# Attention and feed-forward in one program per engine: feed-forward tiles of 128 times of one batch, and their first steps placed in the last attention cycles

## What is computed

```python
x = _layernorm(x + attention(x))        # 16 heads, latent 32, rope, causal softmax over 512 times
x = _layernorm(x + fp4_ffn(x))          # h = silu(q(x) @ q(w_gate).T) * (q(x) @ q(w_up).T);  q(h) @ q(w_down).T, width 704
x = _layernorm(x + recurrence(x))       # tanh state over the 512 times, in order
x = _layernorm(x + channel_mix(x))      # x, and x one time earlier
```

## Time and profile before

| | us |
|---|---|
| median of 3 runs (lowest, highest) | 2320.34 (2317.63, 2322.99) |
| the profiled execution's own time | 2320.48 |
| its span | 2318.7 |
| PE, DVE, ACT, POOL busy in the span | 2209.4, 1706.9, 1060.6, 1187.8 |
| mean granted TensorE clock | 0.979 |

### The profile page before, as it was taken

The page is one execution under the profiler, slowest core; times in us unless marked ns, Lnnn a source line. Parts: engine busy times, 40 slices in busy tenths (PEclk is TensorE's granted clock), DMA queues, the critical chain, the costliest instruction groups (busy, mean ns, idle before and its releaser), DMA issues. The chain is left out here.

```text
span 2318.7 us, 90879 instructions
## 1 busy us (share of the span) xinstructions
PE 2209.4 (95%) x36556; PEld 1542.3 (67%) x36556; DVE 1706.9 (74%) x4854; ACT 1060.6 (46%) x2707; POOL 1187.8 (51%) x1674
## 2 busy tenths in 40 slices
PE   6999999999999999959999999997999999997997
PEld 3556665556655555536777777776888888885775
DVE  3788888888887777749999999982555555454997
ACT  2656565655666665532222222231444444442444
POOL 3555555655555555525666666662444444441333
PEclk8999999999999999989999999997999999998999
DMA  2211111111111111120100000100101011011232
GB/s 92 91 56 64 57 65 65 65 63 58 57 64 65 65 61 60 52 69 22 33 32 32 32 32 32 34 20 29 32 32 36 32 34 33 32 32 46 84 95 77
DMA packets 101627, 117.73 MB, mean 51 GB/s; under 512 B 10672, under 2 KB 80080, under 8 KB 101456
## 3 DMA queue, kind: packets, MB, share of 16 engines
q1 hardware_dynamic: 101456, 115.44, 15.1%
HBM read 48.29 MB, written 33.55 MB: 35 GB/s over the span
## 5 line engine op out<-in xcount | busy, mean ns | idle before, releaser
L1474 ACT ACTIVATE r_state<-ps_state 128x64 f32<-128x64 f32 x1024 | 228.6, 223 | 295.8 <-PE ps_state L1573 290.7
L1570 PE MATMUL ps_state<-r_state,later_pairs_a 64*64 64x32 f32 x8192 | 334.4, 219 | 19.4 <-ACT r_state L1474 12.5
L1570 PEld LDWEIGHTS ps_state<-r_state,later_pairs_a 64*64 64x64 f32 x8192 | 295.2, 135 | 79.2 <-issue 60.7
L1573 PE MATMUL ps_state<-r_state,later_pairs_a 64*64 64x32 f32 x8192 | 334.6, 220 | 2.8 <-issue 2.8
L423 DVE CUSTOM_DVE_ANT_0 ps_near<-ps_near,mask 128x512 f32<-128x512 f32 (+1 forms) x512 | 270.5, 589 | 89.5 <-PE ps_near L519 89.3
L295 POOL TENSOR_SCALAR_AFFINE_SELECT probsT<-probsT 128x512 f32<-128x512 f32 x256 | 159.8, 636 | 271.2 <-ACT probsT L406 168.0
L1573 PEld LDWEIGHTS ps_state<-r_state,later_pairs_a 64*64 64x64 f32 x8192 | 288.8, 135 | 3.1 <-issue 3.1
L423 DVE CUSTOM_DVE_ANT_0 ps_far<-ps_far,mask 128x384 f32<-128x384 f32 (+1 forms) x512 | 198.3, 457 | 32.7 <-PE ps_far L519 31.7
L1158 POOL TENSOR_TENSOR f_fp<-f_rounded,f_scale 128x960 f32<-128x960 f32 (+2 forms) x67 | 117.3, 1750 | 166.2 <-DVE f_rounded L1248 166.2
L527 PE MATMUL ps_far<-Q,K 32*128 32x256 f32 (+2 forms) x1536 | 180.9, 415 | 1.2 <-ACT probsT L403 0.5
L1181 ACT ACTIVATE f_silu<-ps_gate 128x704 f32<-128x704 f32 x64 | 48.5, 758 | 288.5 <-PE ps_gate L1273 288.5
(11 more groups left out here) (213 smaller groups left out, 5401.1 us busy)
## 6 DMA issues: line engine op xcount, KB each, us to landing
q_swap<-q_sin SPq DMA_DIRECT2D x128, 128.0 KB, 2.1
k_swap<-k_sin SPq DMA_DIRECT2D x128, 128.0 KB, 2.1
xT<-in_xT_dram SPq DMA_DIRECT2D x16, 512.0 KB, 3.6
xtok<-in_x_dram SPq DMA_DIRECT2D x16, 512.0 KB, 3.8
x_rows<-x SPq DMA_DIRECT2D x16, 512.0 KB, 2.9
f_x<-x_rows SPq DMA_DIRECT2D x64, 128.0 KB, 2.0
x_rows<-f_x SPq DMA_DIRECT2D x64, 128.0 KB, 1.7
r_x<-x_rows SPq DMA_DIRECT2D x64, 128.0 KB, 2.1
```

Of the source, the lines that this page charges most:

```text
L1474: nc.scalar.activation(state[:, j % 2, banks, :, t, 0, :], sums[:, j % 2, banks, :, now], ACT.Tanh).then_inc(state_ready[t], 1)
L1570: nc.tensor.matmul(sums[half(v), j % 2, stays, c, now], A[half(v), 3 * q, c, :], last[half(v), stays, c, :], start=False, stop=True, skip_ ...
L1573: out = nc.tensor.matmul(sums[half(1 - v), j % 2, changes, c, now], A[half(v), 3 * q + 1 + was, c, :], last[half(v), changes, c, :], start ...
```

## The change

What it does:

1. One block for both layers. Each of the two functions now returns its five programs; `Steps` holds the place that an engine has reached in the feed-forward steps, and `feed.to(n)` writes out the steps up to n-1 where it is called inside the attention program. The barrier between the two layers, and SP's wait for all x1 stores ahead of it, are gone. x1 is read under the attention's own semaphore `x1_stored`.
2. A tile is now 128 times of one batch: tile n is times 128(n//16) to 128(n//16)+127 of batch n%16. So the first 16 tiles need one finished batch each, and tiles 0 to 7 can be loaded long before the attention ends. The rows of a tile in x1 and x2 now lie 16 KB apart (before: 1 KB, one after another); the 128 pieces of a load or store are 1 KB each in both.
3. The first feed-forward steps go to these places:
   - SP: steps -4 to 3 (8 loads of x) in cycle 62; later loads wait for z and for `x1_stored`.
   - DVE: steps -4 to -1 in cycle 63 behind y; step 0 at the end of cycle 64, step 1 of cycle 65, step 2 of cycle 67 (behind the second half of z), then the statistics of batch 15, then step 3 and on.
   - POOL: steps -4 and -3 ahead of the first mask of cycle 63, -2 and -1 behind it; steps 0 to 2 at the end of cycle 65, and behind them the norm of batch 15.
   - ACT: step -1 (copy of xT) ahead of the far Exps of cycle 63, step 0 behind them; steps 1 and 2 at the end of cycle 65, and behind them x1 of batch 15; step 3 behind that.
   - PE: step -1 (turn of x) ahead of the far scores of cycle 63; step 0 in cycle 64 ahead of the last PV, after the Exps of far[0] and far[1] (its up product waits for all Exps); step 1 in cycle 65 ahead of the output projections; step 2 in cycle 67 after all of z.
4. PSUM: `ps_hT` takes the place of near[0] and near[1], `ps_down` near[2], `ps_xT` near[3], `ps_gate` far[0] and far[1], `ps_up` far[2] and far[3]. The last half projection goes to near[2] instead of near[1], and no longer waits for the first half of z.
5. The tensors of the attention are laid out in another order, so that those of the feed-forward layer lie on ones no longer in use. SP's feed-forward steps are written out instead of looped. The weights of the later layers are loaded in step 12 instead of step 0.

The diff without what is only indented anew (the order of the SBUF tensors, which carries nothing of the text below, is left out too):

```diff
+class Steps:
+    def __init__(self, engine, step, tiles, unroll, lead, lag):
+        self.engine, self.step, self.tiles, self.unroll = engine, step, tiles, unroll
+        self.at, self.end = -lead, tiles + lag
+    def to(self, end):
+        unroll = self.unroll
+        while self.at < end:
+            if self.at == unroll and end >= self.tiles - unroll > unroll:
+                with self.engine.Fori(1, self.tiles // unroll - 1) as k:
+                    for j in range(unroll):
+                        self.step(k * unroll + j, j, k)
+                self.at = self.tiles - unroll
+            else:
+                self.step(self.at, self.at % unroll, self.at // unroll)
+                self.at += 1
...
+        def sync(sp, feed):
...
+                    if is_cycle(i, g, CYCLES - 2):
+                        sp.wait_ge(quantiser.copied, len(quantiser.fills))
+                        feed.to(4)
...
-                sp.wait_ge(x1_stored, 16 * BATCH)
...
+        def gpsimd(pool, feed):
...
+                    if is_cycle(i, g, CYCLES - 1):
+                        feed.to(-2)
                     if runs(i, g, 0):
                         pool.wait_ge(exped, cyc(12, i, g, 4))
                         hide(mine, 0).then_inc(masked, 1)
+                    if is_cycle(i, g, CYCLES - 1):
+                        feed.to(0)
...
+                    if is_cycle(i, g, CYCLES + 1):
+                        feed.to(3)
...
+        def scalar(act, feed):
...
                         nc.scalar.copy(yT[:], near[0]).then_inc(yT_out, 1)
+                    if is_cycle(i, g, CYCLES - 1):
+                        feed.to(0)
...
                             nc.scalar.activation(mine[:, t, AT[1]:AT[1] + SEQ], far[t], ACT.Exp).then_inc(exped, 1)
+                    if is_cycle(i, g, CYCLES - 1):
+                        feed.to(1)
+                    if is_cycle(i, g, CYCLES + 1):
+                        feed.to(3)
...
+        def vector(dve, feed):
...
+                    if is_cycle(i, g, CYCLES - 1):
+                        feed.to(0)
...
-                            add_tokens(near[1], 1, 2 * i)
+                        add_tokens(near[2] if i == BATCH else near[1], 1, 2 * i)
+                    if is_cycle(i, g, CYCLES):
+                        feed.to(1)
+                    elif is_cycle(i, g, CYCLES + 1):
+                        feed.to(2)
+                    elif is_cycle(i, g, CYCLES + 3):
+                        feed.to(3)
...
+        def tensor(pe, feed):
...
+                if is_cycle(i, g, CYCLES):
+                    pe.wait_ge(exped, 12 * CYCLES - 2)
+                    feed.to(1)
...
-                        elif g == 3:
-                            pe.wait_ge(z_added, 2 * i - 1)
                         pe.wait_ge(yf_out, 2 * i)
-                        out_projection(near[1], g - 2)
+                    out_projection(near[2] if g == 3 and i == BATCH else near[1], g - 2)
+                if is_cycle(i, g, CYCLES - 1):
+                    pe.wait_ge(exped, cyc(12, i, g, 4))
+                    feed.to(0)
+                elif is_cycle(i, g, CYCLES + 1):
+                    feed.to(2)
+                elif is_cycle(i, g, CYCLES + 3):
+                    pe.wait_ge(z_added, 2 * BATCH)
+                    feed.to(3)
...
+    def rows(dram, n):
+        return dram[n // BATCH * P:(n // BATCH + 1) * P, n % BATCH, :]
...
+            if i == LATER:
                         later_weights.load(sp, a)
...
+                n = i + 4
+                if n >= UNROLL:
+                    sp.wait_ge(z_added, n + 1 - UNROLL)
+                if n < BATCH:
+                    sp.wait_ge(x1_stored, 16 * (n + 1))
+                sp.dma_start(x[:, n % UNROLL, :], rows(x1_dram, n)).then_inc(x_loaded[n % UNROLL], 16)
...
             if exists(i, 0):
                 if later(i, 0, 1):
                     pe.wait_ge(h_done, i)
+                else:
+                    pe.wait_ge(*attended)
                 up(j, ps_up, FFN).then_inc(up_full, 1)
```

More of the change, by code:

```diff
@@ L819, in attention_arrays @@
+            straight(step)
+        return Programs(sync, gpsimd, scalar, vector, tensor), early, x1_stored, (exped, 12 * CYCLES)
 def attention_arrays(inputs):
@@ new lines, in fp4_ffn @@
+    rstd = sb("rstd", [P, 2])
+    minus = sb("minus", [P, 2])
+    shift = sb("shift", [P, 2])
+    x2 = sb("x2", [P, 2, DIM])
+    amax, scale, over, recip = (sb(name, [P, 2, BLOCKS]) for name in ("amax", "scale", "over", "recip"))
+    ratio, power, rounded, fp4 = (sb(name, [P, 2, WIDE]) for name in ("ratio", "power", "rounded", "fp4"))
+    x_loaded = [sem(f"x_loaded{s}") for s in range(UNROLL)]
+    x_amax, h_amax, over_ready, recip_ready, scale_ready = (sem(n) for n in ("x_amax", "h_amax", "over_ready", "recip_ready", "scale_ready"))
@@ new lines, in fp4_ffn, with exists, later, rounds @@
+    set_up, mv_ready = sem("set_up"), sem("mv_ready")
+    veps_ready, rstd_ready, shift_ready = sem("veps_ready"), sem("rstd_ready"), sem("shift_ready")
+    x2_ready = sem("x2_ready")
+    x2_stored = [sem(f"x2_stored{s}") for s in range(2)]
+    FIRST = -2
+    def exists(i, d):
+        return not isinstance(i, int) or 0 <= i + d < TILES
+    def later(i, d, n):
+        return not isinstance(i, int) or i + d >= n
+    def rounds(i):
+        return exists(i, 2) or exists(i, -1)
+    def scales(x_step, h_step):
+        if not isinstance(x_step, int):
+            return x_step + h_step + 5
+        return min(max(x_step + 4, 0), TILES) + min(max(h_step + 1, 0), TILES)
@@ L1950, in program, with _ @@
         kept = FfnWeights(nc, ctx)
-        attention(nc, a, x1, kept)
+        attend, early, x1_stored, attended = attention(nc, ctx, a, x1, kept)
         weights = LaterWeights(nc, ctx)
-        fp4_ffn(nc, a, kept, weights, rows(x1), rows(x2))
+        memory = ctx.enter_context(ExitStack())
+        memory.enter_context(nc.sbuf_tensor("gap", [P, (early - nc.sbuf_base) // 4], F32))
+        feed = fp4_ffn(nc, ctx, memory, a, kept, weights, x1, x1_stored, attended, x2)
+        with nc.Block() as block:
+            @block.sync
+            def _(sp):
+                steps = feed.sync(sp)
+                attend.sync(sp, steps)
+                steps.finish()
+            @block.gpsimd
+            def _(pool):
+                steps = feed.gpsimd(pool)
+                attend.gpsimd(pool, steps)
+                steps.finish()
+            @block.scalar
+            def _(act):
+                steps = feed.scalar(act)
+                attend.scalar(act, steps)
+                steps.finish()
+            @block.vector
+            def _(dve):
+                steps = feed.vector(dve)
+                attend.vector(dve, steps)
+                steps.finish()
+            @block.tensor
+            def _(pe):
+                steps = feed.tensor(pe)
+                attend.tensor(pe, steps)
+                steps.finish()
+        memory.close()
         recurrence(nc, kept.ident, weights, rows(x2), rows(x3))
```

1511 lines of the change are left out of this document (738 added, 773 removed).

## The result

| | before | after |
|---|---|---|
| median of 4 runs, us (lowest, highest) | 2320.43 (2317.63, 2322.99) | 2296.55 (2295.46, 2297.93) |
| ratio (95% interval) | | 0.9898 (0.9881 to 0.9915) |
| the profiled execution: time, span | 2320.48, 2318.7 | 2295.46, 2293.7 |
| mean granted TensorE clock | 0.979 | 0.985 |

The kernel became 23.9 us faster by the medians; the forecast was 25.1 less, 2295.2 with a range of 2291.5 to 2302.

A forecast was written before the change was run, and what follows sets the result against it. PE bounds the dense feed-forward at 8.20 us a tile, unchanged; only the stretch before gate product 4 shrinks. Its start moves from 1070.09 to 1044.9, 25.2 us less, giving 2295.2 us, range 2291.5 to 2302.

The forecast's parts named there:

- The bound: Dense feed-forward: PE sets the pace at 8.20 us a tile, DVE close behind at 8.03; unchanged from gate 4 on.
- Cycle 63: Late attention: steps -4 to -1 fit DVE's and POOL's idle time; far Exps end at 1007.65 instead of 1007.40.
- Cycle 64: Gate 0 at 1006.75; PV starts 3.0 us late behind tile 0's products, takes 2.36 not 4.06, ends 1.26 later.
- rival A: Clock falls inside the filled stretch: one fall costs 1.7 us, two 3.4 (2298.6), low throughout 2313; chance 0.20.
- Cycle 65 and z: Attention's tail: PE and DVE arrive together; z done at 1026.9, attention ends 4.3 us later, gate 2 at 1026.95.
- Step 3: Silu 3 starts 3.0 us late behind x1 of batch 15; 1.55 lost at down product 1, gate 4 at 1044.9.
- The sum: Gate product 4 starts at 1044.9 instead of 1070.09, 25.2 us less; 2295.3 against the profiled 2320.48, forecast median 2295.2.
- B: Fuller overlap: x1 of batch 15 early enough for silu 3 (1.55 back), shorter hand-overs (about 1); 2292.7; chance 0.10.
- C: Inserted steps only queue behind the attention's tail, leaving 14 us of gain from barrier, pipeline fill and clock; 2306.5; chance 0.06.
- D: Tile loads late in steady state: 0.5 us beyond 16.4 costs 28 us, about 2323; chance 0.04 including similar unseen cost.

The follow-up runs named there:

- e4: Changed kernel with x1 of batch 15 behind feed-forward step 3 on ACT instead of ahead; median 2296.52 us, ratio 0.9890 to the kernel before.
- e5: e4 with PE also waiting for the attention's z behind gate product 2, not ahead of it; median 2298.27 us, ratio 0.9897 to the kernel before.
- e7: Changed kernel with PV of cycle 63 ahead of feed-forward step 0 on PE, not behind it; median 2301.08 us, ratio 0.9916 to the kernel before.
- e1: Changed kernel with DVE's, POOL's, ACT's and PE's feed-forward steps all behind the attention, new tiles and early loads kept; median 2313.17 us, ratio 0.9965 to before.
- e3: Kernel before with only tiles of one batch (rows 16 KB apart) and SP's steps written out; median 2321.66 us, ratio 0.9999.
- e6: e1 with the old contiguous tiles, so the first load waits for all x1 stores; median 2323.10 us, ratio 1.0016 to the kernel before.
- e2: Changed kernel with only steps -4 to -1 inside cycle 63, the other steps behind the attention; median 2308.07 us, ratio 0.9955 to the kernel before.
- e8: Kernel before with twelve unused matmuls on PE ahead of gate 0, to raise the clock; median 2318.89 us, ratio 0.9990.

## Why the prediction was right

**The bound.** Right. From gate 4 to gate 63 are 483.89 us after and 483.90 before: nothing of the dense part moved. All that was won in the stretch lies ahead of gate 4.

**Cycle 63.** The prediction had the far Exps slip by 0.22 and gate 0 1.2 us behind their start (1005.55 to 1006.75); measured from their start, gate 0 came after 1.14. The steps on DVE and POOL fitted in. In absolute times both were some 1.6 us later than predicted, since PV of cycle 62 ran at the lower clock, ahead of every changed instruction of PE.

**Cycle 64.** PV was predicted 6.15 us behind the far Exps' start with 2.36 us at full clock; it started 6.29 behind and took 2.36. This was the step with the largest doubt, and the subject of rival A. In the changed kernel, its repeat, e4 and e5 the clock was 1.00 over the whole stretch.

**Cycle 65 and z.** Gate 1 was forecast at 11.75 behind the Exps, measured 11.75; z complete at 21.35, measured 21.27; gate 2 at 21.4, measured 21.33. PE and DVE arrived together, as said: z held PE for 0.87.

**Step 3.** Gate 3 at 29.6, measured 29.63. x1 of batch 15 was forecast from 33.08 to 35.15, measured 33.07 to 35.15; silu 3 started where it ended, 35.06. Down product 1 at 36.75, measured 36.58, gate 4 at 39.35, measured 39.28. e4 took the wait away and won 1.45 where the prediction had 1.55.

**The sum.** The stretch was forecast to shrink by 25.4 (64.76 - 39.35) and shrank by 25.48. In the two profiled executions gate 4 is 23.6 earlier, as the later start of the stretch (1007.21 against 1005.33) took 1.9; behind the layer's last gate product the new kernel gained 1.4. Both lie within what executions of one kernel differ by: between the two profiles of the changed kernel the start of the stretch differs by 5.2 us and the part behind the last gate product by 2.0. Over all profiles here the start lies between 1005.33 and 1012.71, for kernels with and without the change. So the size of the stretch was forecast by its mechanism, while a whole time only 1.3 us from the forecast is partly luck. The recurrence and what follows took 739.3 us, against 740.8 before.

**The rivals.** A did not happen inside the stretch in the four profiles named above; in e7, which differs only in an order, it did. B did not happen in the changed kernel, where silu 3 waited as forecast. e5 takes this wait and that for z away and wins 2.4 us, close to B's 2.5, though B's second term was meant for shorter hand-overs and not for z. C was sized at 14 us of gain for steps that only queue behind the tail; e1, which is that case, kept 8.9 us in the stretch. Both its terms were too large: PE's idle time in the stretch fell by 9.7 us (64.76 - 40.02 against 55.85 - 40.82), not by 11.9, and the lower clock, where 2 us had been counted as won, cost 0.8 more than before. D did not happen, and e3 shows no late load. The Trainium skill's warning on row pitches of large powers of two ("DMA: Bandwidth & Descriptors", "Latency and other measured facts") is not seen at 16 KB: 2.1 us of landing at the median after, 2.0 before.

**What stays open.** Why e6's median is above that of before although its stretch is shorter; why e2's times gain less than its stretch; what the clock alone would give, since e8 did not keep it up; and how the 23.9 us of the medians and the 25.5 of the stretch differ, if they do: the interval of the ratio stands for 20 to 28 us.

## What to carry to other kernels

Where one layer's chain of short hops ends and the next layer's pipeline fills, put the next layer's first steps into the gaps, and choose its tiles so that the first ones need only what is long finished. Here the tiles alone brought 8.2 us, and the places inside the old chain, which need such tiles, another 16.6. Reckon such a stretch as one list per engine with the old chain's hops kept, and look for every instruction of the old chain that now waits, or now blocks a queue (x1 ahead of silu); measured from a common anchor such a sum held to 0.2 us at eight places. A filled stretch can pay twice: here up to 4.2 of the 25.5 us were clock that PE kept.

## What the runs showed of the hardware

The granted clock falls for a few us in the attention's last cycles in every profile here. The kernel before, e3 and e8 have the same code there, and the falls lie at different places: in PV of cycle 63 alone (4.06 us), in PV of cycles 62 and 63 (4.06 and 3.31), in PV of cycle 62 alone (4.46). The two profiles of the changed kernel show it at the same place. Windows of 1 us in the kernel after, about PV of cycle 62:

```profile
997.00:998.00 1.00, 0.31 (x4) 0.21 (x8) 0.90 (x3) 1.00 (x3) 0.00 (x0) 0.88 0.00 0
998.00:999.00 1.00, 1.00 (x8) 0.27 (x4) 0.93 (x3) 1.00 (x3) 0.00 (x0) 0.50 0.00 0
```

It fell to the lower level behind a gap of 0.82 us, while the gap of the same size ahead of the same product did nothing in the earlier trace rows, and the gaps of 0.71 and 0.81 us around yT did nothing in the four filled profiles with the clock at 1.00. The other way round, PV of cycle 63 behind the same idle 2.81 us took 4.06 us in the kernel before, 3.36 in e1, 3.96 in e2, 3.31 in e3, 4.05 in e6, 3.62 in e7 and 2.36 in e8. One such fall cost 1.0 to 2.1 us in PV (against 2.36), 1.6 to 2.4 in gate 0 (4.22 to 5.06 against 2.63, where PE had been idle before it) and 1.4 to 1.7 in the layer's last down product. Their number and places make much of the spread between executions: in e3 the stretch begins 7.4 us later than in the kernel before, and PE was busy 6.3 us longer ahead of it with the same products. The Trainium skill ("TensorE: Matmul & The Clock Gate", "Part 1") says that the chip's check of how busy PE is runs freely, so that the same code sees the clock change at different places from run to run; the rows of the kernel before, e3 and e8 fit that.
